# Two shifted-window attention layers on one core: roots moved to GpSimd, output projection in three rounded parts, one TensorE loop, a new bias table, exponentials over pairs of banks

## The reference

```
x  -> group norm over 32 groups of 8 channels and all tokens (the layer's input)
xs  = roll(x, (-4, -4));  windows of 8 x 8: 4 windows per image, N = 64 tokens each
q, k, v = xw @ Wq.T, xw @ Wk.T, xw @ Wv.T + bv           # 16 heads of 16 channels
qn, kn  = q / max(|q|, 1e-12), k / max(|k|, 1e-12)       # cosine attention
logits  = qn @ kn.T * exp(min(logit_scale, log 100))
table   = relu(coords @ cpb_w1.T + cpb_b1) @ cpb_w2.T    # 225 entries x 16 heads
logits += 16 * sigmoid(table[relative position index]);  masked pairs -> -inf
z = softmax(logits) @ v @ Wo.T + bo;  roll back;  x = x + z   # the residual
```

## Time and profile before

| what | value |
|---|---|
| median of 3 runs | 893.68 us |
| the profiled execution | 888.09 us |
| its span, first to last instruction | 885.6 us |
| mean granted TensorE clock | 0.956 |
| PE busy, PEld busy | 767.5 us, 654.2 us |
| DVE, ACT, POOL busy | 606.6, 453.1, 457.3 us |

### The profile page before, as it was taken

The page is one execution under the profiler, slowest core; times in us unless marked ns, Lnnn a source line. Parts: engine busy times, 40 slices in busy tenths (PEclk is TensorE's granted clock), DMA queues, the critical chain, the costliest instruction groups (busy, mean ns, idle before and its releaser), DMA issues.

```text
span 885.6 us, 38114 instructions
## 1 busy us (share of the span) xinstructions
PE 767.5 (87%) x15258; PEld 654.2 (74%) x15258; DVE 606.6 (68%) x1641; ACT 453.1 (51%) x848; POOL 457.3 (52%) x584
## 2 busy tenths in 40 slices
PE   3086899999999999997999999999999999999985
PEld 2065778777877787776788887787778777788874
DVE  5164677777767777776777777777777777777641
ACT  2143555555555555653555555555655555555540
POOL 2015546555655665555466555565556555665540
PEclk9576999999999999998999999999999999999995
DMA  5706520000000000000000000000000000000000
GB/s 113 137 12 95 163 61 0 0 0 0 0 0 0 0 0 0 0 3 2 3 3 4 15 26 15 24 24 24 24 12 24 24 24 12 24 26 27 26 28 28
DMA packets 17197, 22.13 MB, mean 25 GB/s; under 512 B 7097, under 2 KB 8418, under 8 KB 17122
## 3 DMA queue, kind: packets, MB, share of 16 engines
q1 hardware_dynamic: 16578, 20.31, 8.8%
q10 hardware_dynamic: 544, 0.79, 0.3%
HBM read 12.68 MB, written 8.42 MB: 24 GB/s over the span
## 4 chain that ended last, share of the span: by engine, by line
PE 62%; DVE 15%; issue 9%; ACT 9%; SPq 3%; DMA 1%; ACTq 1%; DVEq 0%
PE ps_qk L365 21%; PE ps_mix L477 15%; PE ps_qk L489 12%; PE ps_score L450 9%; DVE ps_score L709 5%; ACT squares L553 4%; ACT seed L597 3%; PE ps_mix L467 2%; PE ps_score L410 2%; DVE ps_score L725 2%; DVE ps_score L727 2%; DVE ps_score L729 2%; ACT q_own L575 1%; DVE exp_bias L688 1%; DVE g_off L746 1%
## 5 line engine op out<-in xcount | busy, mean ns | idle before, releaser
L913 POOL TENSOR_TENSOR probs<-probs,exp_bias 128x512 f32<-128x512 f32 x256 | 326.4, 1306 | 267.5 <-ACT probs L612 257.5
L612 ACT ACTIVATE probs<-ps_score,lower 128x512 f32<-128x512 f32 x256 | 155.1, 689 | 128.2 <-PE ps_score L450 128.2
L365 PE MATMUL ps_qk<-w_qk,xn 128*128 128x512 f32 x768 | 205.0, 418 | 0.6 <-POOL xn L892 0.6
L365 PEld LDWEIGHTS ps_qk<-w_qk,xn 128*128 128x128 f32 x768 | 147.3, 199 | 32.3 <-POOL xn L892 0.7
L477 PE MATMUL ps_mix<-v_ones,probs 64*64 64x17 f32 x8064 | 134.3, 209 | 6.5 <-issue 6.5
L477 PEld LDWEIGHTS ps_mix<-v_ones,probs 64*64 64x64 f32 x8064 | 127.6, 136 | 8.7 <-issue 6.7
L553 ACT ACTIVATE squares<-ps_qk 128x512 f32<-128x512 f32 x128 | 76.6, 599 | 109.3 <-PE ps_qk L365 109.3
L398 PE MATMUL ps_mix<-mixed,w_o 128*128 128x256 f32 x512 | 131.0, 400 | 1.4 <-ACT mixed L567 1.4
L450 PE MATMUL ps_score<-q_own,k_rows 32*64 32x128 f32 x4096 | 78.4, 281 | 57.9 <-DVE g_off L746 56.8
L489 PE MATMUL ps_qk<-w_v,xn 128*128 128x256 f32 x768 | 109.4, 293 | 20.3 <-DVE unit L761 20.3
L450 PEld LDWEIGHTS ps_score<-q_own,k_rows 32*64 32x64 f32 x4096 | 63.4, 132 | 82.5 <-DVE g_off L746 50.1
(11 more groups left out here) (74 smaller groups left out, 766.7 us busy)
## 6 DMA issues: line engine op xcount, KB each, us to landing
x_all<-in_x SPq DMA_DIRECT2D x32, 256.0 KB, 2.9
out<-x_out SPq DMA_DIRECT2D x32, 256.0 KB, 2.0
bias_rev<-table_scratch SPq DMA_DIRECT2D x32, 56.5 KB
probs<-in_L_matrices ACTq DMA_DIRECT2D x1, 512.0 KB, 3.7
x_out<-in_L_matrices SPq DMA_DIRECT2D x1, 512.0 KB, 12.0
w_o<-in_L_matrices SPq DMA_DIRECT2D x4, 128.0 KB
probs<-in_L_matrices ACTq DMA_DIRECT2D x1, 256.0 KB, 4.2
allowed<-in_L_matrices SPq DMA_DIRECT2D x1, 256.0 KB, 11.7
```

The costliest lines, as they stand in the source:

```text
L365: last = nc.tensor.matmul(ps_qk[:, e, :], xn[:, px, t.parity, c, e * P:(e + 1) * P], w_qk[:, pw, t.layer, c, :], start=(c == 0 and i == 0) ...
L612: nc.scalar.activation(probs[:, t.parity, r, :, :, :, :].rearrange("p e c a n -> p (e c a n)"), ps_score[:, r, :], ACT.Exp, bias=lower[:, ...
L913: nc.gpsimd.tensor_tensor(pr, pr, exp_bias[:, t.layer, r, :, :, :, :].rearrange("p e c a n -> p (e c a n)"), ALU.mult).then_inc(weighted, 1)
```

## The change

Seven edits come together.

1. **Roots on GpSimd.** The Newton step moves from VectorE to GpSimd in four operations on SBUF tiles (`sums_sq`, `refined`, `root`, `threes`), plus `g_off`; `rnorm` and `g_inv` go. `make_unit` reads `root` itself; the logit scale is put in by `keep_k`, whose copy becomes a multiplication by `scales`. `normalise` moves from VectorE to ScalarE (Identity with scale and bias). `score` loses the two waits quoted above. ScalarE does both `keep_q` ahead of Ln and Exp.
2. **Three-part output.** `mixed` and `w_o` become float32r pairs; `project_out` is 12 float32r matmuls, of which the last 4 wait for `keep_rest`, a new VectorE subtraction.
3. **TensorE order and loop.** `mix` comes before `project_v`, and TensorE's loop runs from j = 4 to 61 over both layers. For that the split weights have one buffer for both layers and are replaced at j = 31, 32 and 34.
4. **Bias table.** Heads lie side by side; table to HBM and back is 2 + 2 DMAs per layer and one 128-partition multiplication per (e, c), at j = 0 and, for layer 1, one each at j = 28 to 31.
5. **Exponentials over pairs of banks**: 2 ScalarE operations of 1024 columns per image instead of 4 of 512.
6. **Loads.** Images 0 to 3 are issued ahead of the table's way, images 4 and 5 right behind it; weights of layer 1 have tiles of their own.
7. **Constants** that need the identity are made in VectorE's iteration -1.

The core of the diff:

```diff
-            some(-WARM, 4)
-            for layer in range(LAYERS):
-                first = (4, IMAGES + 6)[layer]
-                last = IMAGES * (layer + 1) - 6
+            some(-WARM, loops[0][0])
+            for n, (first, last) in enumerate(loops):
+                rest = loops[n + 1][0] if n + 1 < len(loops) else JOBS + 4
...
@@ project_out
+                pe.wait_ge(mixed_hi, t.count(1, 1))
+                for c in range(CC):
+                    for a in range(2):
+                        for part in range(2):
+                            nc.tensor.matmul(z_cols[:, c, :], w_o[:, part, a, c * P:(c + 1) * P], mixed[:, 0, a, :],
+                                             start=(c + a + part == 0), stop=False, skip_group_check=True)
                 pe.wait_ge(mixed_ready, t.count(1, 1))
                 for c in range(CC):
                     for a in range(2):
-                        last = nc.tensor.matmul(z_cols[:, c, :], w_o[:, t.layer, a, c * P:(c + 1) * P], mixed[:, a, :],
-                                                start=(a == 0), stop=(a == 1), skip_group_check=True)
+                        last = nc.tensor.matmul(z_cols[:, c, :], w_o[:, 0, a, c * P:(c + 1) * P], mixed[:, 1, a, :],
+                                                start=False, stop=(a == 1), skip_group_check=True)
...
@@ score
-                past(pe, exped, t.count(4, 0))
-                if job(j, base, 0) is not None:
-                    pe.wait_ge(rnorm_ready, job(j, base, 0).count(1, 1))
-                if job(j, base, 2) is not None:
-                    pe.wait_ge(gn_scaled, job(j, base, 2).count(2, 2))
+                past(pe, exped, t.count(2, 0))
...
-                project_v(now)
-                mix(j, base, older)
+                mix(j, base, older)
+                project_v(now)
...
-            both_passes(pe, iteration)
+            both_passes(pe, iteration, ((4, JOBS - 2),))
...
@@ ScalarE
+            def normalise(u):
+                act.wait_ge(gn_offset, u.count(1, 1))
+                past(act, xn_ready, u.count(1, 0))
+                for c in range(CC):
+                    nc.scalar.activation(xn32[:, c, :], x_all[:, bass.ds(u.image, 1), c, :].rearrange("p o t -> p (o t)"), ACT.Identity,
+                                         bias=g_off[:, c:c + 1], scale=root[:, 2 * NORMS + c:2 * NORMS + c + 1]).then_inc(xn32_ready, 1)
...
@@ VectorE
+            def keep_rest(t):
+                dve.wait_ge(mixed_hi, t.count(1, 1))
+                past(dve, z_done, t.count(1, 0))
+                nc.vector.tensor_tensor(mixed[:, 1, :, :], back_cols, mixed[:, 0, :, :], ALU.subtract).then_inc(mixed_ready, 1)
...
@@ GpSimd
+            def newton(j, base):
+                at = root_columns(t, u)
+                pool.wait_ge(seeded, chain(base, 1, 1))
+                nc.gpsimd.tensor_tensor(refined[:, at], sums_sq[:, at], seed[:, at], ALU.mult).then_inc(newton_step, 1)
+                step(1)
+                nc.gpsimd.tensor_tensor(refined[:, at], refined[:, at], seed[:, at], ALU.mult).then_inc(newton_step, 1)
+                step(2)
+                nc.gpsimd.tensor_tensor(refined[:, at], threes[:, at], refined[:, at], ALU.subtract).then_inc(newton_step, 1)
+                step(3)
+                nc.gpsimd.tensor_tensor(root[:, at], refined[:, at], seed[:, at], ALU.mult).then_inc(newton_step, 1)
+                step(4)
+                    nc.gpsimd.tensor_tensor(g_off[:, :], root[:, 2 * NORMS:], neg_mean[:, :], ALU.mult).then_inc(gn_offset, 1)
```

More of the change, by code:

```diff
@@ L213, in past, with run @@
                 engine.wait_ge(semaphore, value)
-        def run(engine, iteration, exact):
+        def run(engine, iteration, exact, loops):
             def some(a, b):
@@ L229, in run, with both_passes @@
                         iteration(first + parity, Job(half, parity, None, exact))
-                some(last, last + (12, 10)[layer])
-        def both_passes(engine, iteration):
-            run(engine, iteration, 0)
+                some(last, rest)
+        def both_passes(engine, iteration, loops=((4, 28), (IMAGES + 4, 60))):
+            run(engine, iteration, 0, loops)
             engine.wait_ge(flag_ready, 1)
@@ L236, in both_passes @@
             with engine.If(again != 0):
-                run(engine, iteration, 1)
+                run(engine, iteration, 1, loops)
         def job(j, base, k):
@@ L260, in load_x @@
                     return
[L261 to L262 removed]
+                past(sp, x_moved[t.parity], t.moves(16))
+                sp.dma_start(x_all[:, bass.ds(t.image, 1), :, :], x[:, bass.ds(t.image, 1), :, :]).then_inc(x_moved[t.parity], 16)
             def store_x(t):
@@ L316, in iteration @@
                 if j == -WARM and not base.exact:
-                    load_table(1)
+                    keep_table()
                     spread_bias(0)
-                    rows = weights[1]["matrices"].rearrange("(c p) o -> p c o", p=P)
-                    sp.dma_start(w_qk_in[1], rows[:, :, 0:2 * D]).then_inc(qk_in[1], 16)
-                    sp.dma_start(w_v_in[1], rows[:, :, 2 * D:3 * D]).then_inc(v_in[1], 16)
-                    load_out()
-                if j == 3 and not base.exact:
+                    load_x(Job(2, 0, 0, 0))
@@ L324, in iteration @@
+                    load_x(Job(2, 1, 0, 0))
+                    load_out(0)
+                    load_out(1)
+                if j >= 0:
+                    load_x(job(j, base, PREFETCH))
+                if j == 2 and not base.exact:
+                    load_qkv(1)
+                    sp.wait_ge(bias_ready, 2 * CC)
                     spread_bias(1)
+                    sp.dma_start(hide, consts["consts32"][:, FIRST_COLS:FIRST_COLS + CONST_COLS["hide"]].rearrange("p (e m) -> p e m", m=N)).then_inc(hide_in, 16)
@@ L546, in _, with rectify_hidden, find_table @@
-            act.wait_ge(filled, FILLS)
+            def rectify_hidden():
+                for l in range(LAYERS):
+                    act.wait_ge(hidden_done, l + 1)
+                    nc.scalar.activation(hidden[:, l, :], ps_score[:, l, 0:REL * REL], ACT.Relu).then_inc(hidden_ready, 1)
+                act.wait_ge(table_done, 2 * LAYERS)
+                nc.scalar.activation(table[:, :, :, :], table_cols, ACT.Exp, scale=-1.0).then_inc(table_exp, 1)
+            def find_table():
+                act.wait_ge(table_inv, 2)
+                nc.scalar.activation(table[:, :, :, :], table[:, :, :, :], ACT.Exp, bias=act_bias[0:ENTRIES, 0:1], scale=BIAS_TOP).then_inc(table_ready, 1)
```

488 lines of the change are left out of this document (248 added, 240 removed).

## The result

The changed kernel takes **770.8 us** (median of four runs, 770.2 to 771.9) against 893.6; the ratio is 0.864 with a 95% interval from 0.859 to 0.868. I forecast 792, with a range of 775 to 828. The profiled execution took 770.32 and its span is 768.5.

A forecast was written before the change was run, and what follows sets the result against it. TensorE, busy 87%, was taken as the bound. Job 6 at 94.3, 648.3 to job 63 and 42.7 to the end gave a span of 785.3, with profile and median factors 792.8, stated as 792 us, range 775 to 828.

The forecast's parts named there:

- Scores: Before the scores: TensorE's 0.79 us wait for g_off goes, with q ready at 5.8 and k at 6.02.
- second wait: Rival before the scores and nearby: thin margins slip, TensorE gets back 0.5 us per image, 822 us; chance 0.17.
- Output projection: TensorE's project_out: 12 float32r matmuls take 1.56 us against 1.99, gain 0.43; the wait for keep_rest is just covered.
- Order, roots on GpSimd: Mix before v: 0.13 us charged for the residual; GpSimd operations of 0.33 leave v covered by 0.8.
- slower rival: GpSimd's Newton becomes the bound and v waits for unit: about 970 us; chance 0.03.
- steady sum: One TensorE iteration: 12.43 - 0.79 - 0.43 + 0.13 = 11.34 us per image, a gain of 1.09.
- One loop: TensorE's middle iterations: six more back edges of 0.35 us cost +2.1; fetch of written-out code counted as 0.
- Start: Before job 6: sum -31.2 us, of which -18.1 for the wait for image 3; job 6 starts at 94.3.
- second rival: The start keeps its holes, as loads stay bunched: gain 12 us instead of 31, so 811; chance 0.13.
- End: Job 63 to the end: 44.9 us less 1 and 0.4 for each of three more output projections, 42.7.
- From profile to median: Added to the span of 785.3 us: 2.5 for the profiled execution, then 0.63% for the median, giving 792.8.
- better: Case with no bubble and all holes gone: 775 us; chance 0.05.

The follow-up runs named there:

- e3: Kernel before, with VectorE's Newton results in SBUF instead of the scores' fourth bank and VectorE's two waits for the exponentials removed: 846.2 us, ratio 0.957.
- e4: Kernel before with the edits of e3, plus mix before v and the residual before Newton: 847.8 us.
- e2: Changed kernel with the output projection in plain float32 (8 matmuls, no split operand, no keep_rest): 790.5 us.
- e6: Changed kernel with four more GpSimd operations of 66 columns in each image's Newton chain: 837.1 us.
- e1: Changed kernel with v projected before mix again, all else as changed: 884.9 us, ratio to the kernel before 1.001.
- e5: Changed kernel with Newton's four operations and g_off back on VectorE, behind the residual: 777.7 us.
- e10: Changed kernel with TensorE's loop split in two again (jobs 4 to 27 and 36 to 59), the jobs between written out: 783.5 us.
- e8: Kernel before, with the loads of images 3 and 4 issued ahead of the output weights and biases: 871.6 us, ratio 0.972.
- e13: Changed kernel with TensorE's two loops, and v ahead of mix in the written-out jobs alone (28 to 35, 60 to 63): 791.9 us.

## Why the prediction was right where it was, and where it failed

*Scores* (no second wait): right. e3 and e4 show what it hangs on. Both keep Ln and Exp among the two `keep_q`, and `q_own` is late by 0.14 to 0.36 in layer 0's loop in either order of v and mix; the changed kernel does both `keep_q` first, and it isn't.

*Output projection*: 1.61 instead of 1.56; the split wait costs nothing. Against the 1.99 of before that is 0.38 per image, against the 1.93 of e2 0.32, where I had 0.43.

*Order, roots on GpSimd*: right. Operation 322 ns (330), half 1 of `unit` at 8.65 (8.9), slack 0.8 (0.8, and e6 shows it one for one). The bubble behind the scores that I had at 0.13 is 0.15 on average in layer 0's loop and 0.27 in layer 1's. In jobs 28 to 35, which VectorE has written out, it is 0.00 and 0.08, and the residual begins 0.04 after the projection ends, against 0.16 and 0.27 in VectorE's two loops. So this margin was the real one: it is why layer 1's periods are 11.12 and 11.27. The slower rival asked for 0.8 us per operation. But I named the move as one of several steps, and e1 and e5 say what it is worth: the order is 1.9 per image with the roots on GpSimd, 0.43 with them on VectorE (e4 against e3, the residual moved too); the engine by itself is worth nothing in the steady part. The gain from 12.45 to 11.08 per image in layer 0 is 0.50 for the roots out of the scores' bank (e3), 0.43 for the order (e4), 0.32 for the output projection (e2), and the remaining 0.11 for all else (against e4, `q_own` is no longer late, and the bubble has come).

**The step that failed is the steady sum**: a gain of 1.09 per image, measured 1.34 in layer 0 (1.2 in layer 1). The waits and edits that it names came out near: 0.79 of wait, 0.38 for the projection (0.43), a bubble of 0.15 (0.13). What it had wrong is that three of TensorE's own pieces, carried over as fixed, got shorter, because v and not mix now stands in front of the back edge and the group sum:

| piece, per image in layer 0's loop | before | after |
|---|---|---|
| group sum to q/k | 0.24 | 0.14 |
| mix, with the edge that before follows it | 2.47 | 2.30 |
| v, with the edge that now follows it | 1.57 | 1.53 |

That is 0.31 per image at nothing in the sum. e1 brings the first two back in the changed kernel, e4 takes them from the kernel before, e3, which keeps mix last, leaves them: it is shown from both sides that what stands before the edge decides its cost. Why is not shown. A likely reading is that the twelve long matmuls of v still occupy TensorE while the branch and the next instructions are handled, and the 126 short ones of mix don't.

By stretches against 11.34 per job: jobs 7 to 27 -5.4, 28 to 35 -2.8, 36 to 59 (11.2 on average) -3.4, 60 to 62 -1.5, job 6 at the low clock +1.5, and the 2.1 that I added for *One loop* -2.1. That is the 13.6, to a tenth. The other parts of the miss from 792.8 to 770.8 are 3.9 at the end and 5.2 from profile to median, less 0.7 at the start.

*One loop* had the wrong sign as an edit, though it is a small term of the miss. I took the written-out code as free because the kernel before shows it so, and charged 2.1 for six more back edges of 0.35. It is eight passes through a loop more, not six; 0.35 is right where mix comes last, and with v last they cost nothing. The written-out code was free because v stood between scores and mix. With the new order two loops cost 16 (e10), so the single loop is part of what the gain rests on. The Trainium skill (Runtime: NRT & Kernel Launch, Instruction fetch mechanics) says that a taken branch whose target lies outside the instructions at hand forces a fetch, and that kernels prefer full unrolling where possible. These runs go the other way: nothing for an edge behind v, 0.32 behind mix, 16 us for twelve jobs written out.

*Start*: 95.0 against 94.3. Its largest term is confirmed by e8 (18.2 of 18.1), and job 0 begins at 16.9 (16.4). No run isolates the other terms, which make up 11 us, and the start scatters from 91.9 to 95.1 over six traces, so an agreement within 1 us is in part luck. The second rival's holes remained as four of about 1 us, with periods of 12.1 to 14.5; there, and in the bubble before mix, some gain is left.

*End*: 38.8 instead of 42.7, 6.2 less than before rather than 2.2. From one transposing back to the next, and to the end, the four steps got shorter by 2.5, 0.4, 1.9 and 1.3. Of the first, 1.4 is a wait for `o_rows` that v, now behind mix, covers. The rest no run isolates; nine traces of the changed kernel and its near variants have ends from 36.8 to 39.8.

*From profile to median*: 5.2 of the 22 us between my sum and the time. The 0.63% by which the kernel before was slower in its median than in its profile is scatter of its own (its runs reach from 877 to 903 in these batches); the changed kernel's first four runs lie within 0.2%, its later ones within 1.1%. I should have left that factor out, and widened the range for it.

*Range*: I let the bounds below be set by the forecast's own terms and gave "better" 0.05. The pieces that I called TensorE's own work had no bound below, and they are what went past it.

## What to carry to other kernels

Order the bound engine's work so that what waits longest comes last, and try its longest instructions ahead of its branch and its small steps: the same edit here hid a chain of 1.6 us, the whole back edge and 0.1 of the step behind it. Read the cost of an edge from the step that holds it, with and without; the difference of two periods holds all that alternates. Then move work to a slower engine freely, up to the slack, and measure the slack by lengthening the chain. When the bound engine issues hundreds of short instructions in one piece, keep it in a loop whose code has already run.

## What the runs showed of the hardware

- Behind the start, code executed for the first time cost TensorE holes of 0.7 to 1.4 us in mix (126 matmuls, 2.05 us) in some jobs when the scores directly precede it (e10, e4), and none when 12 matmuls of 256 columns stand between (e13's twelve written-out jobs, the kernel before, e3).
- A loop's back edge costs TensorE 0.32 us behind 126 short matmuls (the kernel before, e1) and nothing behind the 12 of v (the changed kernel, e4).
- With a wait of 0.75 in each image the granted clock fell to 1.2 GHz for a while in some images and not in others (e6): 0.81 per image were waited, about 1.0 per image lost between job 6 and job 63.
- The group sum (two matmuls of four columns) takes 0.24 to the next instruction's start behind short matmuls and 0.14 behind long ones.
- Two exponentials of 1024 columns take 2.12, four of 512 take 2.42; it doesn't matter which, because neither ScalarE nor GpSimd is late.
